# Layer 0 of a four-layer graph network: rows also loaded transposed and centred there, means spread by transfers, no TensorE transposes for it after the first pairs

## What is computed

```python
h = jnp.maximum(_layernorm(x, axis=-1), 0.0)
x = x + _L0_gnn_ref(h, adj, L0_gnn_W, L0_gnn_b)   # deg*(h@Wi + b) + adj @ (h@Wj)
h = jnp.maximum(_layernorm(x, axis=-1), 0.0)
x = x + _L1_gnn_ref(...)                          # one-head attention, width 256
h = jnp.maximum(_layernorm(x, axis=-1), 0.0)
x = x + _L2_gnn_ref(...)                          # one-head attention, width 128, and h itself
h = jnp.maximum(_layernorm(x, axis=-1), 0.0)
x = x + _L3_gnn_ref(...)                          # 8-head attention, 4 projections
```

## Time and profile before

| | |
|---|---|
| median of the executions | 1260.56 us |
| span of the profiled execution | 1270.7 us |
| TensorE busy | 98% |
| VectorE, ScalarE, GpSimd busy | 84%, 82%, 84% |
| DMA engines busy | about a fifth |

### The profile page before, as it was taken

One profiled execution on the slowest core, in us unless ns is written; L12 is line 12 of the kernel. 1 busy time (PEld: TensorE's weight loads), 2 busy tenths in 40 slices (PEclk: granted clock), 3 DMA queues, 4 the chain that ended last, 5 costly groups with the idle time before them and its releaser, 6 DMA issues. The chain is left out here.

```text
span 1270.7 us, 43666 instructions
## 1 busy us (share of the span) xinstructions
PE 1244.1 (98%) x12253; PEld 1143.5 (90%) x12253; DVE 1073.1 (84%) x5137; ACT 1042.1 (82%) x3911; POOL 1066.2 (84%) x1914
## 2 busy tenths in 40 slices
PE   8899999999999999999999999999999999999997
PEld 6789999999999999999899999899999989999986
DVE  5788888888988888888888888888988888888883
ACT  3578888888888888888788888788888888898996
POOL 6879888888888888888788888889888888887773
PEclk8999999999999999999999999999999999999998
DMA  4011221222222321221211222322222312211000
GB/s 127 26 23 22 52 43 36 52 36 43 52 39 40 52 45 35 51 47 32 52 32 47 48 35 48 48 34 50 48 36 47 48 31 52 48 27 31 19 19 34
DMA packets 70604, 53.59 MB, mean 42 GB/s; under 512 B 20704, under 2 KB 70368, under 8 KB 70368
## 3 DMA queue, kind: packets, MB, share of 16 engines
q1 hardware_dynamic: 67888, 49.09, 20.0%
q10 hardware_dynamic: 2480, 1.71, 0.5%
HBM read 33.89 MB, written 16.89 MB: 40 GB/s over the span
## 5 line engine op out<-in xcount | busy, mean ns | idle before, releaser
L795 ACT ACTIVATE exps<-masked,nmax 128x128 f32<-128x128 f32 x1024 | 397.5, 398 | 0.0
L335 POOL TENSOR_SCALAR y<-x,nm,rstd 128x256 f32<-128x256 f32 x512 | 281.0, 557 | 23.4 <-issue 21.8
L364 POOL TENSOR_TENSOR probs<-exps,rsum 128x512 f32<-128x512 f32 x256 | 263.5, 1041 | 10.4 <-PE bank L1019 5.6
L577 DVE CUSTOM_DVE_ANT_0 masked<-bank,mask 128x128 f32<-128x128 f32 x1024 | 227.8, 284 | 2.9 <-PE bank L1011 2.8
L795 ACT ACTIVATION_READ_ACCUMULATOR exps<-masked,nmax 128x1 f32 x1024 | 202.3, 198 | 0.0
L486 DVE BATCH_NORM_STATS2 stats<-x 128x6 f32<-128x256 f32 x512 | 190.8, 414 | 8.7 <-DMA x<-in_x 7.2
L901 PE MATMUL bank<-w_hi,ht_hi 128*128 128x512 f32 (+1 forms) x512 | 187.7, 367 | 2.1 <-DVE ht_lo L524 2.1
L327 POOL TENSOR_TENSOR rstd<-veps,power 128x2 f32<-128x2 f32 x256 | 182.8, 714 | 0.1
L524 DVE SCALAR_TENSOR_TENSOR ht_lo<-bank,ht_hi 128x512 fp32r<-128x512 f32 x192 | 131.0, 682 | 57.1 <-ACT ht_hi L726 56.8
L903 PE MATMUL bank<-w_hi,ht_lo 128*128 128x512 f32 (+1 forms) x512 | 175.6, 343 | 0.0
L902 PE MATMUL bank<-w_lo,ht_hi 128*128 128x512 f32 (+1 forms) x512 | 175.3, 342 | 0.0
(11 more groups left out here) (122 smaller groups left out, 3737.5 us busy)
## 6 DMA issues: line engine op xcount, KB each, us to landing
x<-in_x SPq DMA_DIRECT2D x64, 256.0 KB, 5.0
out<-x SPq DMA_DIRECT2D x64, 256.0 KB, 6.2
db<-rows SPq DMA_DIRECT2D x110, 128.0 KB, 4.1
rows<-dst SPq DMA_DIRECT2D x110, 1.0 KB, 4.1
probs<-in_w0t ACTq DMA_DIRECT2D x1, 256.0 KB, 5.6
probs<-in_w0t SPq DMA_DIRECT2D x1, 256.0 KB, 6.7
probs<-in_w1t ACTq DMA_DIRECT2D x1, 256.0 KB, 6.7
exps<-in_wot SPq DMA_DIRECT2D x1, 256.0 KB, 7.4
```

The source lines that it names most:

```text
L335: last = pool.tensor_scalar(y[i][:, b, g], src[:, bx, g], nm[i][:, s, g:g + 1], rstd[i][:, s, g:g + 1], ALU.add, ALU.mult)
L364: pool.tensor_tensor(probs3[:, p % BUFFERS["probs3"], j], exps3[:, p % BUFFERS["exps3"], j], rsum3[:, s, j].unsqueeze(2).to_broadcast([P, ...
L577: last = dve.tensor_tensor_reduce(masked3[:, b, j, i], bank_of(f"sc{j}")[:, i * P:(i + 1) * P], mask[:], scale=-1.0, scalar=-MASKED, op0=A ...
L795: last = act.activation(exps3[:, b, j, i], masked3[:, p % BUFFERS["masked3"], j, i], ACT.Exp, bias=nmax3[:, s, j, i:i + 1], scale=-1.0, ac ...
```

## The change

For pairs from the fifth on (`ROWS_FIRST` = 4), the host hands over `x` a second time with each pair's rows transposed (`xt_pairs`). The kernel loads both forms. The mean of each row leaves `mv0` by a 1 KB write and comes back for all partitions by a 128 KB read, as for layers 1 and 2. GpSimd subtracts it from the transposed rows (`u0`), ScalarE applies the ReLU twice, once exactly into PSUM bank 7 (`h0`) and once rounded (`h0t_hi`), and VectorE takes the difference. The division by the deviation moves behind the product with the weights: into the scale of `mj_hi` and `mj_lo`, and into `deg_r`, the degree times the inverse deviation. The first four pairs are still transposed by TensorE, from rows that are centred alone. Adding eps becomes a third group of statistics (count 0, mean 0, eps times 256) that the aggregation takes in, so `veps` is gone in all layers. The tile `x0` gets three buffers.

All lists, lags and banks are new. TensorE's list in one step is now: pt3, wh1, wh0, h3t, m1, (h0t), v, x4_mm, e2t, kt, h2t, x3_mm, qt, pt1, hh_mm, scores, m0, ot_mm, e1t, pt0, h1t, pt2, x2_mm, s0. SyncE's is: row_out2, row_in0, row_in2, load_t, store, row_out1, row_out0, row_in1, load. The latest and earliest lags on TensorE that every pair passes were -2 (h0t) to 7 (x4_mm) and are now -7 (m0) to 2 (x4_mm); `h0t` of the first four pairs has -8.

```diff
-BUFFERS = {"x0": 2, "y0": 2, ...
+ROWS_FIRST = 4
+BUFFERS = {"x0": 3, "xt": 3, "u0": 2, ...
+            def load_transposed(p):
+                b = (p - ROWS_FIRST) % BUFFERS["xt"]
+                u0_made(sp, p - BUFFERS["xt"])
+                sp.dma_start(xt[:, b], xt_pairs[bass.ds(p, 1)].rearrange("o q c g n -> (o q) c g n")).then_inc(xt_in[b], 16)
+
+            def write_mean(p):
...
+                passed(sp, "mv0", p)
...
+                sp.dma_start(rows[0][b], mv[0][:, p % SMALL, 0]).then_inc(row_out[0][b], 16)
+
+            def spread_mean(p):
...
+                sp.dma_start(db[0][:, b], rows[0][b].rearrange("n g -> (n g)").partition_broadcast(P)).then_inc(row_in[0][b], 16)
...
+            pool.memset(stats[:, :, :, :, 6:8], 0.0).then_inc(eps_added, 1)
+            pool.memset(stats[:, :, :, :, 8:9], LN_EPS * D).then_inc(eps_added, 1)
...
-                pool.tensor_scalar(veps[i][:, b], mv[i][:, b, :, 1], LN_EPS, None, ALU.add).then_inc(S[f"veps{i}"], 1)
+                pool.tensor_tensor(deg_r[:, b], rstd[0][:, b], deg[:].to_broadcast([P, G]), ALU.mult).then_inc(S["deg_r"], 1)
+
+            def centre_transposed(p):
...
+                mean = db[0][:, p % 2].rearrange("p (n g) -> p g n", g=G).unsqueeze(1).to_broadcast([P, DC, G, P])
+                pool.tensor_tensor(u0[:, b], xt[:, bt], mean, ALU.subtract).then_inc(S["u0"], 1)
...
-                    last = dve.bn_aggr(mv[i][:, b, g], stats[i][:, b, g])
+                    last = dve.bn_aggr(mv[i][:, b, :, g], stats[:, i, b, g])
...
+            def low_h0(p):
...
+                dve.tensor_tensor(ht0_r[1][:, b].rearrange("p c g n -> p (c g n)"), bank_of("h0")[:],
+                                  ht0_r[0][:, b].rearrange("p c g n -> p (c g n)").bitcast(F32), ALU.subtract).then_inc(S["h0t_lo"], 1)
...
-                dve.tensor_tensor(mj_r[1][:, b, g], bank_of(f"m{g}")[:, D:2 * D], mj_r[0][:, b, g].bitcast(F32), ALU.subtract).then_inc(S[f"mj_lo{g}"], 1)
+                dve.scalar_tensor_tensor(mj_r[1][:, b, g], bank_of(f"m{g}")[:, D:2 * D], rstd[0][:, s, g:g + 1], mj_r[0][:, b, g].bitcast(F32),
+                                         ALU.mult, ALU.subtract).then_inc(S[f"mj_lo{g}"], 1)
...
+            def relu_h0(p):
...
+                act.activation(bank_of("h0")[:], u0[:, p % BUFFERS["u0"]].rearrange("p c g n -> p (c g n)"), ACT.Relu).then_inc(S["h0"], 1)
...
-                act.activation(mj_r[0][:, b, g], bank_of(f"m{g}")[:, D:2 * D], ACT.Copy).then_inc(S[f"mj_hi{g}"], 1)
+                act.activation(mj_r[0][:, b, g], bank_of(f"m{g}")[:, D:2 * D], ACT.Copy, scale=rstd[0][:, s, g:g + 1]).then_inc(S[f"mj_hi{g}"], 1)
```

More of the change, by code:

```diff
@@ L60 @@
-    "h1t": (3, "h1t", ('h1t_lo',)),
-    "sc0": (1, "scores", ('nmax3_0',)),
+    "prepa": (3, "adj_spread", ('adj_rows',)),
+    "pt3": (1, "pt3", ('p3t_3',)),
+    "d2": (5, "d2", ('z2',)),
+    "wh1": (6, "wh1_mm", ('wh1',)),
+    "wh0": (2, "wh0_mm", ('wh0',)),
+    "prep": (4, "products", ('w1_split',)),
+    "zz1": (7, "z1", ('nmax1',)),
+    "h3t": (4, "h3t", ('h3t_lo',)),
+    "m1": (5, "m1", ('mj_lo1', 't0_1')),
+    "h0t": (0, "h0t", ('h0t_lo',)),
+    "v": (6, "v_mm", ('v',)),
+    "x4b": (2, "x4_mm", ('x4',)),
@@ L62 @@
+    "at2": (3, "e2t", ('at2',)),
+    "kt": (4, "kt_mm", ('kt',)),
+    "h2t": (2, "h2t", ('ht2',)),
+    "x3b": (3, "x3_mm", ('x3',)),
+    "qt": (1, "qt_mm", ('qt',)),
+    "d1": (6, "d1", ('z1',)),
+    "pt1": (4, "pt1", ('p3t_1',)),
+    "hh": (0, "hh_mm", ('hh',)),
+    "sc0": (6, "scores", ('nmax3_0',)),
     "sc1": (2, "scores", ('nmax3_1',)),
     "sc2": (5, "scores", ('nmax3_2',)),
-    "sc3": (0, "scores", ('nmax3_3',)),
-    "prepa": (0, "adj_spread", ('adj_rows',)),
-    "ot": (4, "ot_mm", ('ot_lo',)),
@@ L67 @@
-    "at1": (6, "e1t", ('at1',)),
-    "pt1": (3, "pt1", ('p3t_1',)),
-    "h0t": (2, "h0t", ('h0t_lo',)),
-    "x2b": (6, "x2_mm", ('x2',)),
-    "wh0": (5, "wh0_mm", ('wh0',)),
-    "wh1": (1, "wh1_mm", ('wh1',)),
-    "v": (2, "v_mm", ('v',)),
-    "h3t": (5, "h3t", ('h3t_lo',)),
-    "d2": (4, "d2", ('z2',)),
-    "x1b": (3, "s0", ('x1',)),
-    "zz2": (7, "z2", ('nmax2',)),
-    "zz1": (7, "z1", ('nmax1',)),
+    "sc3": (3, "scores", ('nmax3_3',)),
+    "zz2": (7, "z2", ('nmax2',)),
+    "m0": (1, "m0", ('mj_lo0', 't0_0')),
@@ L79 @@
+    "ot": (0, "ot_mm", ('ot_lo',)),
+    "at1": (5, "e1t", ('at1',)),
+    "h0": (7, "h0", ('h0t_lo',)),
+    "pt0": (4, "pt0", ('p3t_0',)),
+    "h1t": (6, "h1t", ('h1t_lo',)),
+    "pt2": (5, "pt2", ('p3t_2',)),
+    "x2b": (2, "x2_mm", ('x2',)),
+    "x1b": (0, "s0", ('x1',)),
 }
@@ L439, in _ @@
-            negative_mean(0, "y0", 0)
-            normalise(0, x0, 0)
+            centre_rows(0)
             for t in range(first_step, last_step):
@@ L1054, in step @@
                     project_transposed("qt", wq_r, t - LAG["qt_mm"])
+                if due(t, "d1") and at_an_end(t - LAG["d1"]):
+                    spread_dst(1, wh, "wh", last_of("wh0", "wh1"), D + 1, t - LAG["d1"])
+                if due(t, "pt1"):
+                    transpose_p3(1, t - LAG["pt1"])
+                if due(t, "hh_mm"):
+                    project2(t - LAG["hh_mm"])
+                if due(t, "scores"):
+                    scores(t - LAG["scores"])
                 if due(t, "m0"):
```

562 lines of the change are left out of this document (307 added, 255 removed), and 24 rows, old and new, of the table LAG.

## The result

The changed kernel takes 1312.03 us (median of four executions, 1310.57 to 1315.59) where the kernel before takes 1260.51 in the same session: 1.0408 times as long, 95% interval 1.0391 to 1.0426. The prediction said 1245 and faster. The profiled execution has a span of 1309.0 us, 38.3 more than the profiled one before.

What follows compares the result with a forecast made beforehand. TensorE's queue was taken as the bound: 1260.6 us, less 28.2 (transposes), 3 (bank reuse) and 1 (earlier start), plus 14 (passages) and 2.8 (fill), gives 1245.2 us; 1236 to 1253, overall range 1231 to 1268.

Steps and rivals of the forecast that it cites:

- e1t: TensorE task directly behind `ot_mm`: 0.27 us instead of 0.22, read as the cost of leaving quartered use of the array.
- The bound and the distance of steps: Whole kernel: one long TensorE queue sets the time, with scores starting 19.02 us apart per step.
- TensorE's transposes and new order: TensorE: 60 of 64 pairs lose four `h0t` transposes, saving 28.2 us; new step about 18.7 us.
- Passages: TensorE, `m0` between scores and `ot_mm`: a fourth switch between quartered and full array, 0.23 us a step, 14 us.
- The other engines: GpSimd, ScalarE, VectorE: 15.7, 16.8 and about 16.8 us a step, so none becomes the bound by load.
- Fill and drain: Start and end of the kernel: one step more adds 2.8 us, an earlier first pair takes off 1.
- Transfers, "Cost 0": SyncE's queue: layer 1's delayed row trip of 5.3 us is hidden by 0.8 us, so added transfers cost nothing.
- The rule on the fixed part of a transfer: Row trips: the skill's 2.0 us fixed part would hide the trip by 3 us; the measured 4.1 us decides.
- Rival A: TensorE waits on shorter hand-overs, losing 0.2 to 0.4 us a step: 1257 to 1269 us, chance 0.22.
- Rival B: SyncE's queue: the means' spread delays layer 1's loop through `mv0`, `z1` and `nmax1`: 1275 to 1296 us, chance 0.13.
- tell-tale: Layer 1's waits of SyncE for `mv0` and ScalarE for `db`: growth from 6.9 past 60 us would show Rival B.
- wrong altogether: Sign on TensorE: busy under 97% in the middle would mean the whole prediction fails.

Runs made afterwards that it cites:

- second run: Changed kernel with the mean written and read for pairs 4 and 5 only, so layer 0 uses wrong means: 1242.91 us, ratio 0.9871.
- first run: Changed kernel with layer 2's row spread by TensorE for all 64 pairs instead of travelling through memory: 1256.14 us, ratio 0.997.
- twelfth run: Changed kernel with layer 2's rows spread by TensorE for all pairs and `m0` behind `ot_mm`: 1251.16 us, ratio 0.9928.
- seventh run: Changed kernel with the mean's read one step earlier, behind the load at the end of SyncE's step: 1265.75 us, ratio 0.9976.
- ninth run: Changed kernel with the mean's transfers in place but read into an unused tile, `u0` subtracting rows loaded once: 1307.54 us, ratio 1.0386.
- thirteenth: Changed kernel with both of the mean's transfers issued by ScalarE instead of SyncE: 1333.99 us, ratio 1.0546.
- tenth run: Changed kernel with the mean's read one step earlier and its write moved behind layer 1's read: 1353.42 us, ratio 1.0738.
- fifth run: Kernel before the change, with a 128 KB read, 256 KB load and 1 KB write per pair added that nobody waits for: 1301.7 us, ratio 1.0255.
- fifteenth run: Changed kernel with the mean's transfers issued by ScalarE, the read later, behind layer 1's copy of transposed exponentials: 1322.0 us, ratio 1.048.

## Why the prediction was wrong, point by point

- **The bound and the distance of steps: right.** TensorE bounded the kernel before. The 19.02 us from five steps of the chain is 0.1 below the 19.13 of the middle, by five good steps. TensorE's list without any stall is 18.87 us, taken as the sum, over its tasks, of the shortest distance from a task's start to the next one's; the shortest step in the middle is 18.88. The 0.26 us up to 19.13 were waits, part of them for late rows (19.5 us in the whole run).
- **TensorE's transposes and new order: right.** "About 18.7 us" was forecast. The second run's steps are 18.57, the shortest of them 18.55. The transposes are 784, 768 of `y` and 16 of `u`, as said.
- **Passages: the mechanism right, the size too high.** 0.23 us per step was forecast for the fourth passage (bounds 0 and 0.36). The first and twelfth run differ by 0.11 us in locked steps; the slots give 0.15 (`m0` takes 1.60 us between scores and `ot_mm`, 1.50 elsewhere, `e1t` 0.27 instead of 0.22). The Trainium skill's rule (TensorEngine Tiling (Array Packing), § Key Properties: a change of the tiling mode drains TensorE) agrees in sign: the passage costs 7 to 9 us in 1260 (0.11 or 0.15 us on 62 steps). The draining itself no row shows.
- **The other engines: right.** The steps' loads in the middle are 15.7 us on GpSimd, 16.7 on ScalarE and 16.6 on VectorE (870.44, 926.31 and 923.34 times 19.78 / 1100), forecast 15.7, 16.8, 16.8. The rows of the new and changed instructions:

```profile
L371 POOL TENSOR_TENSOR u<-xt,db 128x512 f32<-128x512 f32 x60 | 78.3, 1305 | 134.8 <-issue 134.8
L580 DVE SCALAR_TENSOR_TENSOR mj_lo<-bank,rstd,mj_hi 128x256 fp32r<-128x256 f32 x128 | 60.1, 471 | 1.9 <-ACT mj_hi L828 1.9
L828 ACT ACTIVATE mj_hi<-bank,rstd 128x256 fp32r<-128x256 f32 x128 | 59.3, 463 | 3.8 <-PE bank L1004 3.7
L814 ACT ACTIVATE bank<-u 128x512 f32<-128x512 f32 x60 | 35.9, 598 | 0.0
```

  `u0` takes 1305 ns (1.30 forecast), `mj_lo` 471 (0.47), the new ReLU 598 (0.60). Not costed was `mj_hi`, which takes a scale per row now: 463 ns for 384 before, 0.16 us a step on ScalarE; no run tests its effect.
- **Fill and drain: right in kind.** 2.8 - 1 = 1.8 us forecast, 1.2 measured.
- **Transfers, "Cost 0": this step failed**, and it carries the error: without the mean's trip the kernel takes 1243 us (second run), where 1245 was forecast. That this is within 2 us is partly luck, since the passages were put 5 to 7 us too dear and nothing was put down for waits on rows, of which 8.5 us are left there. The share of the DMA engines was forecast well (0.35, measured 0.37), but it was the wrong question. Three things were left out. First, the prediction followed layer 1's row from `mv0` to `nmax1` and never layer 2's, from `dst2` over SyncE and `z2` and back. Second, it asked whether each trip is hidden for one passage and not what the whole circle takes. The circle's engine part, 11.07 us under the new lists, plus the trip of 7.82 us that the kernel before shows, is 18.89: above TensorE's 18.55, with no new transfer counted. With the 7.21 us of the second run it is 18.28, and TensorE does set the step there; so a trip may take no more than about 7.5 us. That GpSimd, ScalarE and VectorE have 10% to spare didn't help, since the circle waits for their order and not for their load. Third, it took the landing of 4.1 us as a constant. With the mean's 128 KB read between layer 2's write and read, the write takes 3.61 instead of 3.02 us (second run) and the read 5.08 instead of 4.18: 1.5 us in all, and the step grows by 1.2.
- **The rule on the fixed part of a transfer.** The Trainium skill's DMA: Bandwidth & Descriptors, § Anatomy of one DMA, puts it at about 2.0 us; its section is on transfers that GpSimd issues, and these are issued by SyncE. In the second run the rows' 1 KB writes took 3.0 us on average from issue to landing, in the middle never under 2.5; the measured number decides.
- **Rival A** (short hand-overs): not seen. TensorE's waits on `qt`, `ht_lo` or `ot_lo` are absent from the head of the waits; its 38.8 us are on `wh1`, which is late because it stands behind `z2` in ScalarE's list.
- **Rival B** (the spread of the means through SyncE): right in its queue and its sign, given 0.13. It was wrong in its place: `mv0`, `write_mean` and `z1` have slack, since the first run keeps them and loses the delay. It was wrong in its price, 1275 to 1296, since it let the mean's read delay nothing but layer 1. Its tell-tale was layer 1's wait for `db` past 60 us, and this did not come: `z1` waits 21.1 us; layer 2's, which the prediction did not name, are the 117.1. The sign of being "wrong altogether" did hold, TensorE at 96.1% in the middle.

What stays open: of the 1.1% by which the seventh run is slower than the second, the trips' 7.72 against 7.21 us explain the direction; which transfer meets which in each step was not followed. By what mechanism one transfer lengthens another is not shown. No run shortens GpSimd's list between `dst1` and `dst2`, which the circle asks for next to the trip. Nor was it tried to give the mean's spread to TensorE as the first run does for layer 2's row.

## What to carry to other kernels

Where a result leaves for memory and comes back, close the circle: add the trip to the engines' time from its arrival to the next departure, for every such trip and under the new lists, and compare it with the bound's step. A transfer added between the two halves of a trip, or overlapping either, made the trip up to 2.0 us longer here (7.21 to 9.19 us), from SyncE's queue as from ScalarE's, so look for a place where neither is in flight before asking for bandwidth. Follow the engines' part through every list it passes: here it ran through an engine that is busy 77% of the time. And of the waits of a profile the large ones needn't cost: 134.8 us at `u0` cost nearly nothing (ninth run), while TensorE's 38.8 us, the smallest of the first six, are nearly all of the 42.4 us that it idles more than before.

## What the runs showed of the hardware

- A 1 KB write took 3.0 us until its read could be issued, on average, without a mean's read near it (second run). With a 128 KB read issued 0.4 to 0.8 us ahead of it, it took 4.5 and 4.7 (thirteenth and tenth run); with one issued 0.4 us behind it, 3.6 (changed kernel) and 3.2 (fifth run). In the old list layer 1's write, with a 256 KB load issued ahead of it and a store right behind it, took 5.7.
- Two spread reads of 128 KB issued 0.4 us apart: the second took 5.7 us until `z2` started (fifteenth run), 4.2 without the first (second run). The earlier one is lengthened too. In the changed kernel the mean's read, with layer 2's read, a load and a store issued 2.9 to 3.7 us behind it, lands after 6.8 us in the median, at its place in the seventh run after 3.9.
- Issuing a transfer is mostly 0.32 us of SyncE's time, but not always, as the changed kernel's instructions show (duration in ns, least, median, most):

```profile
L298 SPq DMA_DIRECT2D db<-rows x110: 319/320/2727, 84.7 to 1181.0; - x110
```

  One issue took 2.73 us. Only 1 KB writes were issued within 8 us ahead of it (0.4 and 3.0 us ahead). What makes an issue long was not tested.
